# Six-block attention kernel: transfers straight into the float32r stacks, and maxima turned in 32x32 blocks by VectorE

## What is computed

```
scores = q k^T (+ mask or penalty)      256 x 256
attn   = softmax(scores / sqrt(16))
out    = attn v
```

## Time and profile before

| | us |
|---|---|
| median of 3 runs | 2823.91 |
| lowest and highest | 2817.97, 2825.75 |
| the profiled execution | 2822.13 |
| its span, first to last instruction | 2820.3 |
| TensorE, VectorE, ScalarE, GpSimd busy in it | 2653.0, 1816.7, 1554.2, 749.8 |
| mean granted TensorE clock in it | 0.981 of full |

### The profile page before, as it was taken

How to read it: one execution, slowest core, us unless ns; L and a number is a source line. 1 busy time by engine, 2 the same in 40 slices (tenths; PEclk the granted TensorE clock), 3 DMA queues, 4 the chain that set the end, 5 groups by cost and what they waited for, 6 DMA issues and landing times.

```text
span 2820.3 us, 57005 instructions
## 1 busy us (share of the span) xinstructions
PE 2653.0 (94%) x22720; PEld 1958.1 (69%) x22720; DVE 1816.7 (64%) x3629; ACT 1554.2 (55%) x2129; POOL 749.8 (27%) x838
## 2 busy tenths in 40 slices
PE   7999999899999999999998889889999989999999
PEld 5777777567777777766666666666666667777777
DVE  5566666465555565666668888888677775555552
ACT  1333333365555554566656666666676676666653
POOL 0011111133333332332323444554222221111111
...
DMA packets 138362, 177.67 MB, mean 63 GB/s; under 512 B 51747, under 2 KB 58547, under 8 KB 138036
## 3 DMA queue, kind: packets, MB, share of 16 engines
...
## 4 chain that ended last, share of the span: by engine, by line
PE 82%; DVE 9%; ACT 5%; issue 3%; DMA 1%; SPq 0%; POOL 0%; ACTq 0%; DVEq 0%
PE ps_pv L690 10%; PE ps_nat L517 10%; PE ps_misc L749 9%; PE ps_misc L619 9%; PE ps_st L538 8%; PE ps_misc L771 7%; PE ps_misc L645 6%; PE ps_misc L722 4%; DVE mx L1018 4%; ACT pt L854 3%; PE ps_nat L521 2%; PE ps_misc L701 2%; PE ps_st L542 2%; PE ps_misc L614 2%; PE ps_misc L739 2%
## 5 line engine op out<-in xcount | busy, mean ns | idle before, releaser
L854 ACT ACTIVATE pt<-ps_st 128x1024 f32<-128x1024 f32 (+1 forms) x768 | 758.5, 988 | 616.3 <-PE ps_st L542 288.9
L1018 DVE TENSOR_REDUCE mx<-ps_nat 128x4 f32<-128x1024 f32 x640 | 781.0, 1220 | 413.4 <-PE ps_nat L517 267.5
L538 PE MATMUL ps_st<-q_st,k_st 64*128 64x256 f32 (+1 forms) x2560 | 326.1, 333 | 69.9 <-ACT pt L854 66.6
L538 PEld LDWEIGHTS ps_st<-q_st,k_st 64*128 64x128 f32 x2560 | 194.8, 188 | 249.7 <-issue 184.9
L690 PE MATMUL ps_pv<-pt,vaug 128*32 128x256 f32 (+1 forms) x6144 | 361.0, 376 | 0.0
L517 PE MATMUL ps_nat<-k_st,q_st 64*128 64x256 f32 (+1 forms) x2560 | 273.8, 290 | 40.9 <-DVE mx L1018 34.6
L1156 POOL TENSOR_TENSOR rstd<-var,half_pow 128x2 f32<-128x2 f32 x144 | 103.1, 716 | 726.3 <-DVE var L905 724.6
L749 PE MATMUL ps_misc<-xF,weights 128*128 128x256 f32 x1152 | 281.3, 387 | 1.8 <-ACT xF L868 1.5
L1130 POOL DMA_DIRECT2D q_st<-negm_hi x160 | 97.7, 611 | 690.3 <-DVE negm_hi L1028 690.3
L1164 POOL TENSOR_TENSOR xn<-xn,tiles 128x512 f32<-128x512 f32 x128 | 163.8, 1280 | 412.7 <-DVE xn L909 412.4
L690 PEld LDWEIGHTS ps_pv<-pt,vaug 128*32 128x32 f32 x6144 | 179.6, 110 | 123.1 <-issue 10.6
(11 more groups left out here) (117 smaller groups left out, 4082.3 us busy)
## 6 DMA issues: line engine op xcount, KB each, us to landing
qk<-upper SPq DMA_DIRECT2D x320, 256.0 KB, 2.5
qk<-lower SPq DMA_DIRECT2D x160, 256.0 KB, 2.6
...
```

Of the source, the lines that this page charges most:

```text
L538: return nc.tensor.matmul(ps_st[:, j, kh, 0:S - q0], lhs, rhs, start=kh == first, stop=last)
L854: nc.scalar.activation(pt[:, g % PT_SLOTS, :, 0:used], ps_st[:].rearrange("p j a b -> p j (a b)")[:, :, 0:used], ACT.Exp, scale=SCALE).the ...
L1018: last = nc.vector.reduce_max(out, ps_nat[:], AX)
```

## The change

What it does:

- **Stacks.** `raw_q`, `raw_k`, `qcp` and `kcp` are gone. `upper` and `lower` have two buffers (rot), on the space of `qk0` that `raw_q` and `raw_k` had. `qin` and `kin` come in halves: for each four pairs SyncE issues three transfers of 128 KB straight into `q_st` or `k_st`, read as float32, and for q a fourth that writes zeros into the shift rows. Their wait for `st` of unit n - 2 stands on SyncE now. VectorE writes `lower` as float32r. The columns of the projections are permuted so that even partitions hold the first four pairs. `nat` waits for the transfers' semaphores. The constant rows are loaded once, early.
- **Shift.** TensorE's transpose is gone, and nmt with it from the general banks. VectorE makes both parts from `mx` into `shifts` (128x32), transposes that in 32x32 blocks, and four transfers a half (one for each block) move 32 partitions of 32 values: SyncE in stage 0, GpSimd later. The shift rows lie on partitions 31 and 63 of each group of 64, so four partitions with one stride. nmt is 3.2 slots after the half's first nat.
- **Order.** `PRE` and `POST` have new times.

The diff, cut to its core:

```diff
-PEN_R, HI_R, LO_R = 3, 7, 11
+PEN_R, HI_R, LO_R = 3, 31, 63
 PRE = {
...
-    3: [("ldn", 0, -20.3), ("xtr", 0, -14.8), ("ctr", 0, -14.3), ("pq", 0, -10.5), ("qin", 0, -9.95),
-        ("pql", 0, -9.7), ("kin", 0, -9.4), ("pk", 0, -9.15), ("pkl", 0, -8.8), ("pen", 0, -7.2),
-        ("q0b", 0, -7), ("e0", 0, -6.3), ("len", 0, -5.75), ("qcp", 0, -4.1), ("kcp", 0, -3.3),
-        ("qcp", 1, -1.7), ("kcp", 1, 1.1), ("pvv", 0, 1.5)],
+    1: [("ldt", 0, -19.8), ("xtr", 0, -15.65), ("pq", 0, -10.2), ("pql", 0, -9.8), ("pk", 0, -9.6),
+        ("pkl", 0, -9.55), ("kin", 0, -7.8), ("qin", 0, -4.3), ("kin", 1, -2.1), ("pvv", 0, 0.1),
+        ("qin", 1, 3.4)],
+    3: [("ldn", 0, -17.8), ("xtr", 0, -14.8), ("ctr", 0, -14.3), ("pq", 0, -10.5), ("pql", 0, -9.8),
+        ("pk", 0, -9.6), ("pkl", 0, -9.55), ("q0b", 0, -8.1), ("e0", 0, -8), ("len", 0, -7.4),
+        ("pen", 0, -5.1), ("qin", 0, -3), ("kin", 0, -2.6), ("qin", 1, -2.3), ("pen", 1, -1.7),
+        ("kin", 1, -0.8), ("pvv", 0, 1.5)],
-    4: [("xtr", 0, -12.4), ("pq", 0, -11.2), ("pql", 0, -9.8), ("qin", 0, -9.6), ("pk", 0, -9.4),
-        ("pkl", 0, -9), ("kin", 0, -7.35), ("qcp", 0, -6.1), ("kcp", 0, -2.6), ("qcp", 1, -1.6),
-        ("kcp", 1, 0.75), ("pvv", 0, 2.5)],
+    4: [("xtr", 0, -13.6), ("pq", 0, -10.6), ("pql", 0, -10.55), ("pk", 0, -9.8), ("pkl", 0, -8.85),
+        ("qin", 0, -7.5), ("kin", 0, -5.4), ("qin", 1, -2.6), ("kin", 1, -1.2), ("pvv", 0, 1.5)],
...
 POST = {
...
-    4: [("otr", 0, 15.6), ("otr", 1, 17.5), ("ott", 0, 18.55), ("opr", 0, 21.2), ("lnA", 0, 22.1),
+    4: [("otr", 0, 16.6), ("otr", 1, 17.95), ("ott", 0, 18.5), ("opr", 0, 20.3), ("lnA", 0, 24.6),
...
-            add(8 * n + 4 * i + 4.6, "nmt", n, i)
+            add(8 * n + 4 * i + 3.2, "nmt", n, i)
...
-MISC_KINDS = ("nmt", "pq", "pk", ...
+MISC_KINDS = ("pq", "pk", ...
...
+        upper = qk0[:, 0, 1:3].rearrange("p r (k c) s -> p r k (c s)", k=2)
+        lower = qk0[:, 1, 1:3].rearrange("p r (k c) s -> p r k (c s)", k=2)
...
                     elif kind in ("qin", "kin"):
+                        if n >= B + 2:
+                            sp.wait_ge(st_done, nth(("st", n - 2, 4 * i + 3)))
...
+                            sp.dma_start(dst[HI_R:P:LO_R - HI_R], zeros[:].unsqueeze(1).to_broadcast([4, 4, S])).then_inc(done, 16)
...
                         for part, src in enumerate(parts):
                             sp.dma_start(dst[part:P:STEP], src).then_inc(done, 16)
...
                     if attention(n) > 0 and p % 4 == 0:
-                        pe.wait_ge(q_stacked, nth(("qcp", n, p // 4)))
-                        pe.wait_ge(k_stacked, nth(("kcp", n, p // 4)))
+                        pe.wait_ge(q_in[n % 2][p // 4], placed("qin", n, p // 4))
+                        pe.wait_ge(k_in[n % 2][p // 4], placed("kin", n, p // 4))
...
-                    elif kind == "nmt":
-                        pe.wait_ge(max_done, nth(("nat", n, 4 * i + 3)))
-                        bank = open_bank(e)
-                        filled(e, nc.tensor.transpose(bank[0:16, 0:P], mx[:, i, :], ident[:]))
...
-                        nc.scalar.activation(q_st[:, rot, 4 * i:4 * i + 4, :], raw_q[:, 4 * i:4 * i + 4, :],
-                                             ACT.Copy).then_inc(q_stacked, 1)
...
                     elif kind == "nmt":
...
+                        dve.wait_ge(max_done, nth(("nat", n, 4 * i + 3)))
...
+                            link(nc.vector.tensor_scalar(parts[:, :, 0].bitcast(F32R), top, FLOOR, -1.0, ALU.max, ALU.mult))
+                            link(nc.vector.scalar_tensor_tensor(parts[:, :, 1].bitcast(F32R), top, FLOOR, parts[:, :, 0],
+                                                                op0=ALU.max, op1=ALU.add))
+                        nc.vector.transpose(shifts_t[:, i, :], shifts[:, i, :]).then_inc(shifts_made, 1)
...
-                        nc.gpsimd.dma_start(q_st[HI_R:P:GROUP, rot, 4 * i:4 * i + 4, :], negm_hi[:, i, :].bitcast(F32)).then_inc(split_in[rot][i], 16)
...
-                        nc.gpsimd.dma_start(q_st[LO_R:P:GROUP, rot, 4 * i:4 * i + 4, :], maxm_lo[:, i, :]).then_inc(split_in[rot][i], 16)
+                        pool.wait_ge(shifts_made, nth(e))
+                        rows = q_st[HI_R:P:LO_R - HI_R, rot, 4 * i:4 * i + 4, :].bitcast(F32).rearrange("p t (f b s) -> p b t f s", f=2, b=4)
+                        for b in range(4):
+                            nc.gpsimd.dma_start(rows[:, b], shifts_t[32 * b:32 * b + 32, i, :]).then_inc(split_in[rot][i], 16)
```

More of the change, by code:

```diff
@@ L89 @@
+    4: [("xtr", 0, -13.6), ("pq", 0, -10.6), ("pql", 0, -10.55), ("pk", 0, -9.8), ("pkl", 0, -8.85),
+        ("qin", 0, -7.5), ("kin", 0, -5.4), ("qin", 1, -2.6), ("kin", 1, -1.2), ("pvv", 0, 1.5)],
+    5: [("ldn", 0, -24.9), ("clnA", 0, -20.1), ("clnB", 0, -17.4), ("ctr", 0, -14.3), ("xtr", 0, -13.3),
+        ("pq", 0, -10.5), ("pql", 0, -9.3), ("pk", 0, -9.1), ("pkl", 0, -8.6), ("qin", 0, -6.2),
+        ("kin", 0, -3.6), ("kin", 1, -1.5), ("qin", 1, -0.4), ("pvv", 0, 0.4)],
 }
 POST = {
-    0: [("otr", 0, 13.4), ("pb", 0, 15.55), ("otr", 1, 17.2), ("ott", 0, 18.4), ("opr", 0, 20.2),
-        ("lnA", 0, 21.6), ("lnB", 0, 26.8)],
@@ L101 @@
[L101 to L109 removed]
+    0: [("otr", 0, 13.4), ("pb", 0, 15.55), ("otr", 1, 17), ("ott", 0, 18.1), ("opr", 0, 20.5),
+        ("lnA", 0, 21.2), ("lnB", 0, 26.8)],
@@ new lines @@
+    1: [("pb", 0, 8.95), ("otr", 0, 14.3), ("otr", 1, 18.5), ("ott", 0, 18.6), ("opr", 0, 20.6),
+        ("lnA", 0, 20.9), ("lnB", 0, 21.8), ("xff", 0, 25.5), ("ff1", 0, 27.14), ("pb", 1, 27.6),
+        ("ff1", 1, 28.2), ("ff2a", 0, 29), ("ff1", 2, 30.05), ("ff2a", 1, 30.38), ("ff1", 3, 31.2),
+        ("ff2a", 2, 33.56), ("ff2", 0, 34.54), ("lnA", 1, 34.6), ("lnB", 1, 35.5), ("msk", 0, 39.3)],
+    2: [("otr", 0, 12.55), ("otr", 1, 16.15), ("res", 0, 19.05), ("lnA", 0, 21.7), ("lnB", 0, 23.1),
+        ("msk", 0, 28.7)],
@@ L153, in plan @@
     return out
-MISC_KINDS = ("nmt", "pq", "pk", "pvv", "pvt", "ctr", "e0", "otr", "ott", "opr", "xtr", "xff", "ff1", "ff2a", "ff2")
+MISC_KINDS = ("pq", "pk", "pvv", "pvt", "ctr", "e0", "otr", "ott", "opr", "xtr", "xff", "ff1", "ff2a", "ff2")
 RELEASE = {"len": "e0", "pql": "pq", "pkl": "pk"}
@@ L385, in _ @@
                     sp.dma_start(dst[:], t[name]).then_inc(const_loaded, 16)
+                for c in range(2):
+                    sp.dma_start(hT[32 * c:32 * c + 32], t["rows"][c]).then_inc(rows_loaded, 16)
                 for e in win.order:
@@ L391, in _ @@
                     elif kind == "tld":
+                        if i == 1:
+                            sp.wait_ge(rows_loaded, 32)
+                            for c, stack in enumerate((q_st, k_st)):
+                                for r in range(2):
+                                    sp.dma_start(stack[STEP - 1:P:STEP, r].bitcast(F32), hT[32 * c:32 * c + 32]).then_inc(rows_in, 16)
                         lo, hi = 4 * i, min(4 * i + 4, len(TILES))
@@ L626, in _ @@
                         bank = open_bank(e)
-                        for low, part in enumerate((upper[:, 1].bitcast(F32), lower[:, 1])):
+                        for low, part in enumerate((upper[:, rot, 1], lower[:, rot, 1])):
                             for m in range(2):
```

204 lines of the change are left out of this document (87 added, 117 removed).

## The result

The changed kernel takes 2775.5 us at the median of 4 runs (2774.1 to 2780.5), against 2824.8 us for the kernel before on the same chip (2818.0 to 2828.7): ratio 0.983, 95% interval 0.981 to 0.985. The forecast was 2742 us with a range of 2698 to 2808: faster, as foreseen, by 49 us (1.7%) instead of 80.

The account below looks back on a forecast made before the run. TensorE, busy 94%, was taken to bound the kernel, with waits and half clock counting in stages 3 and 4. Terms 16 + 15 + 15 + 22 + 12 = 80 us off 2822.1 gave 2742 us, range 2698 to 2808.

Parts of the forecast that it names:

- The 192 transposes, 16 us: TensorE's transposes of maxima go: 0.11 us each, counted fully in stages 0, 1 and 5, half elsewhere; 16 us.
- Stage 1, 15 us for ott's bank: Stage 1: ott no longer waits for VectorE's ff2 to release a general bank; 0.92 x 16 = 15 us.
- so a bank is free: Stage 1: pk opens and frees its bank far from otr, ff2 and ott, leaving ott one; basis of 15 us.
- Stage 3, 15 us: Stage 3: shorter wait of nat for the maximum, some clock back, less a new slot without work; 1.4 us x 11.
- Stage 4, 22 us: Stage 4: 0.7 us less idle, 0.6 clock back, 0.1 for copies gone before exponentials; 1.4 us x 16 units.
- From stage 0 to 1, 12 us: Transition: unit 17 gets its own half of `upper`, ending idle time and lost clock; 12 of 4.6 + 8.2 us.
- Stage 2, taken as unchanged: Stage 2: the forecast's sum has no separate term for this stage.
- a second slot without work for stage 3 (0.5 us): Stage 3: slot 4 loses its otr and its transpose, a cost of 0.5 us a unit.
- Added costs of nothing: New transfers on SyncE (about 1 us spare) and GpSimd (about 3.9 us spare) were priced at 0.
- 3.9 spare: Stage 4: GpSimd's shift transfers land 6.9 us after nat's start, st needs them at 10.8; about 3.9 us spare.
- 0.1 us more: VectorE: the shift's new operations take 0.1 us more per half, beside TensorE; 0.2 us a unit where VectorE ends waits.
- Rival 2: VectorE ends the waits, its new operations meeting GpSimd's; stages 3 and 4 keep their times: 2794 us, chance 0.22.

Follow-up runs that it names:

- e10_dirold: Kernel before, its old order, with only the direct transfers into the stacks replacing ScalarE's copies; TensorE's transposes of maxima kept: 2811.0 us, ratio 0.997.
- e12_late: e9_order with only the shift moved from 3.2 to 4.6, behind the maximum in VectorE's queue: 2828.1 us, ratio 1.002 to the kernel before.
- e9_order: Both parts (direct transfers and shift) in the old kernel's PRE and POST order, the shift at the early place 3.2: 2868.9 us, ratio 1.017 to the kernel before.
- e3_bank: Changed kernel with ff2's general bank put at the end of the planner's turn when ff2 is done: ratio 0.982 to the kernel before.
- e2_otr: Changed kernel with stage 2's first transpose of outputs (otr 0) moved from 12.55 to 13.05, into slot 5: ratio 0.984 to the kernel before.
- e8_lnb: e2_otr with stage 2's normalisation lnB also moved from 23.1 to 23.95, behind q0's block: ratio 0.986 to the kernel before.

## Why the prediction was right or wrong

**Direction and range** were right, the sum was too large by 31 us, and part of what it hit, it hit by luck: gains at other places made up for a stage that got slower. By its own steps:

- **The 192 transposes, 16 us.** The price of 0.11 us each holds roughly: from e10_dirold to e12_late, which has none, usual units go from 30.8 to 30.7, 35.1 to 35.0 and 34.1 to 33.9 us in stages 0, 1 and 5, 0.1 to 0.2 for two. In stages 2 to 4 nothing of it could be kept apart. The changed kernel's usual units gained more, 30.8 to 30.2 us in stage 0 and 34.1 to 33.7 in stage 5; with both parts in the old order (e9_order) they are 30.6 and 33.9, so the rest came with the new order, which the forecast did not price there.
- **Stage 1, 15 us for ott's bank.** Failed: "so a bank is free". It was free, but the planner's turn does not look for it. The wait stayed at 0.88 us; one unit is 34.99 us for 35.08. e3_bank gave 14.4 us, so the price was right and the step was not.
- **Stage 3, 15 us.** In the usual units 25.6 us at the mean (52nd to 61st) for 27.2, or 1.6 x 11 = 17 us: right in the sum, by luck in the parts. nat's wait for the maximum fell from 1.82 to 0.31 us, further than the 0.7 counted, but st now waits for the exponential a second time in the unit:

```profile
1724.06 0.50 PE L544 MATMUL ps_st<-q_st,k_st 64*128 64x256 f32 x4 [1.02 <-ACT pt L838]
1724.88 0.50 PE L523 MATMUL ps_nat<-k_st,q_st 64*128 64x256 f32 x4 [0.31 <-DVE mx L1004]
...
1728.88 0.50 PE L544 MATMUL ps_st<-q_st,k_st 64*128 64x256 f32 x4 [0.96 <-ACT pt L838]
```

  TensorE's idle time fell only from 27.20 - 24.33 = 2.87 to 25.25 - 22.61 = 2.64 us, and nearly all of the gain is the clock, back at 1.00 in seven of the ten units. The stage as a whole gave 9.1, as its first three units went from 64.9 to 76.9 us.
- **Stage 4, 22 us.** Mis-sized: 36.5. The unit is 19.5 us at a clock of 1.00. Idle time fell from 21.35 - 20.00 = 1.35 to 0.38 us, where 0.7 was counted, and the clock came back whole, 22.56 - 21.35 = 1.2 us, where half was. The third part, TensorE's busy time from 20.00 to 19.13 us, stood in the sum only as the 0.1 for two transposes; how much of it they are was not measured.
- **From stage 0 to 1, 12 us.** Units 14 to 19 fell from 191.3 to 178.8 us: 12.5, as worked out. The clock from 520 to 540 is 0.84, under the 0.9 foreseen.
- **Stage 2, taken as unchanged.** The step that failed most: +26.5 us. The forecast weighed a second slot without work for stage 3 (0.5 us) and did not look at slots 4 and 5 of stage 2. That is 11 us (e2_otr), all of it clock. The rest lies at its ends: unit 35, which still carries stage 1's work, one slot later in the new order, went from 26.2 to 33.6 us, and the last two from 47.0 to 53.8. e9_order, both parts in the old order, has 28.6 and 47.0 there, e12_late 25.9 and 46.4, so both come with the new order; which of its entries does it was not tried, and what e8_lnb took away there came back as other waits.
- **Added costs of nothing.** For SyncE right, no wait of nat for a transfer is in the changed kernel's list of large ones. (The 28 us that the prediction works out for 14 transfers in line takes the 2 us of the Trainium skill, "DMA: Bandwidth & Descriptors", Anatomy of one DMA, which the page gives for transfers that GpSimd issues, while these are SyncE's; the sum did not use it.) For GpSimd right in the new order and wrong as a rule: "3.9 spare" was worked out for stage 4, and in the old order of e12_late st waits 22.8 us. For VectorE "0.1 us more" holds only where GpSimd is quiet: L1017 takes 0.175 us at the median and up to 1.26.
- **The start**, not thought of: 5.6 us, and of no weight.

What was wrong as a whole is the way of counting: the forecast priced what the change takes off TensorE and ScalarE. The runs say that, in the old order, taking it off gives 8 us (the transfers) or costs 15 to 58 (the maxima), and that with both parts the new order is worth 53 to 95 us, by the place that the shift has in the old one. Both parts in the old order are no faster than the kernel before (1.002 at best). The tables of PRE and POST, read there as a detail of the change, were what turned it into a gain. Rival 2's mechanism, VectorE held by GpSimd in its new operations, is real, and with its place in the queue cost the old order 41 us; in the new one it hardly meets stages 3 and 4 (L1017 is held twice there in 64), the 14 times that L1016 is held in stage 2 are there in e2_otr's faster stage too, and its 2794 us did not come. The Trainium skill ("GPSIMD Engine Reference", 1. Specifications) says that GpSimd's SBUF interface is contended by VectorE instructions with two SBUF inputs or in a 2-port mode. The trace agrees: L1017 with two SBUF inputs was held up to 1.26 us, while the maximum, which reads PSUM, took 1.18 (L993 above) beside a GpSimd operation and 1.22 otherwise. L1016, with one SBUF input, was held too, up to 1.14 us; whether it ran in a 2-port mode no run here shows.
